# Two groups' activations turned by transfers instead of by TensorE, gates made later, weights tested in 8 bits

## What is computed

```
# experts (after the first layernorm); ensembles holds an expert's number per key, weights its share
h = relu(einsum('edi,bsi->bsed', proj_in, x))     # 8 experts, 256 -> 512
o = einsum('eid,bsed->bsei', proj_out, h)         # 512 -> 256
gate = einsum('bks,bkse->bse', weights, one_hot(ensembles, 8))
x = layernorm(x + einsum('bsei,bse->bsi', o, gate))
# feed-forward: h1_w and h2_w (the "H weights", 1024 x 1024) hold -8, 0 and 8 here
h = silu(tlin(x, w1_w, w1_s)) * tlin(x, w2_w, w2_s)
h = gelu(tlin(h, h1_w, h1_s)); h = gelu(tlin(h, h2_w, h2_s))
x = layernorm(x + tlin(h, w3_w, w3_s))
```

## Time and profile before

| | |
|---|---|
| median of 3 runs | 755.44 us (755.1 to 755.63) |
| profiled execution | 756.6 us, of which its span from the first to the last instruction is 754.8 us |
| TensorE's granted clock over the span | 0.998 |
| busy in the span | TensorE 745.3, VectorE 597.0, ScalarE 433.8, GpSimd 245.2 us |
| the first four steps (experts 0 and 1) | from about 103 to 194 us |
| the three pair passes | from about 194 to 455 us |
| the feed-forward block | from about 455 us to the end |

### The profile page before, as it was taken

The page is one execution under the profiler, slowest core; times in us unless marked ns, Lnnn a source line. Parts: engine busy times, 40 slices in busy tenths (PEclk is TensorE's granted clock), DMA queues, the critical chain, the costliest instruction groups (busy, mean ns, idle before and its releaser), DMA issues.

```text
span 754.8 us, 11840 instructions
## 1 busy us (share of the span) xinstructions
PE 745.3 (99%) x3699; PEld 630.5 (84%) x3699; DVE 597.0 (79%) x1308; ACT 433.8 (57%) x843; POOL 245.2 (32%) x278
## 2 busy tenths in 40 slices
PE   8999999999999999999999999999999999999996
PEld 6888888888888888888888888888888988888886
DVE  4789979876698999989866667894996649969466
ACT  5888743444465655556443338475676465657573
POOL 2776243233574755747443231000000300100003
PEclk9999999999999999999999999999999999999999
DMA  7900000003445345362452011035435101373201
GB/s 247 324 2 0 2 1 1 1 1 89 177 154 169 132 132 188 105 209 97 140 223 57 28 46 47 0 138 170 168 126 181 57 1 40 129 224 119 104 1 60
DMA packets 31707, 77.15 MB, mean 102 GB/s; under 512 B 8736, under 2 KB 13472, under 8 KB 27808
## 3 DMA queue, kind: packets, MB, share of 16 engines
q1 hardware_dynamic: 31360, 76.18, 29.8%
q10 hardware_dynamic: 288, 0.26, 0.2%
HBM read 58.08 MB, written 16.78 MB: 99 GB/s over the span
## 4 chain that ended last, share of the span: by engine, by line
PE 96%; DMA 1%; DVE 1%; ACT 1%; POOL 1%; issue 0%; SPq 0%; DVEq 0%; ACTq 0%
PE bank L1387 16%; PE bank L1537 13%; PE bank L1538 13%; PE bank L1236 9%; PE bank L1271 8%; PE bank L1365 8%; PE bank L1366 8%; PE bank L1370 8%; PE bank L1386 6%; PE bank L1390 2%; PE bank L1545 1%; PE bank L1544 1%; DMA wp_lo_f<-in_wproj 1%; PE bank L1254 0%; PE bank L1255 0%; PE bank L1259 0%
## 5 line engine op out<-in xcount | busy, mean ns | idle before, releaser
L1387 PE MATMUL bank<-wx_both,hx_hi 128*128 128x512 f32 x512 | 191.4, 397 | 0.0
L989 ACT ACTIVATE hx_hi<-bank 128x512 fp32r<-128x512 f32 x128 | 76.4, 597 | 175.4 <-PE bank L1370 174.2
L1537 PE MATMUL bank<-hring,wring 128*128 128x512 f32 x448 | 174.3, 389 | 0.0
L1538 PE MATMUL bank<-part_r,wring 128*128 128x512 f32 x448 | 174.3, 389 | 0.0
L720 POOL TENSOR_TENSOR x_tok<-right,x_tok 128x256 f32<-128x256 f32 x128 | 94.7, 740 | 172.0 <-ACT right L996 167.4
L2036 DVE TENSOR_TENSOR part_r<-part_f,hring 128x512 fp32r<-128x512 f32 x144 | 95.4, 686 | 42.4 <-ACT hring L1146 41.7
L1809 DVE SCALAR_TENSOR_TENSOR hx_lo<-bank,hx_hi 128x512 fp32r<-128x512 f32 x128 | 87.7, 686 | 51.4 <-ACT hx_hi L989 50.1
L1387 PEld LDWEIGHTS bank<-wx_both,hx_hi 128*128 128x128 f32 x512 | 96.0, 188 | 16.7
L1386 PE MATMUL bank<-wx_both,hx_lo 128*128 128x256 f32 x384 | 108.6, 283 | 0.0
L1538 PEld LDWEIGHTS bank<-part_r,wring 128*128 128x128 f32 x448 | 84.1, 188 | 17.5
L1537 PEld LDWEIGHTS bank<-hring,wring 128*128 128x128 f32 x448 | 84.1, 188 | 17.4
(11 more groups left out here) (209 smaller groups left out, 1415.1 us busy)
## 6 DMA issues: line engine op xcount, KB each, us to landing
wring<-h_dram SPq DMA_DIRECT2D x28, 1024.0 KB, 4.8
wx_raw<-in_wx SPq DMA_DIRECT2D x16, 512.0 KB, 7.8
raw_quads<-in_wffn SPq DMA_DIRECT2D x16, 512.0 KB, 5.7
h_dram<-sums SPq DMA_DIRECT2D x8, 1024.0 KB, 4.2
h_dram<-raw_quads SPq DMA_DIRECT2D x8, 512.0 KB, 6.6
stage<-in_wffn SPq DMA_DIRECT2D x12, 256.0 KB, 2.7
x_tok<-in_x SPq DMA_DIRECT2D x1, 2048.0 KB, 12.0
h_dram<-raw_quads SPq DMA_DIRECT2D x8, 256.0 KB, 6.8
```

The source lines that it names most:

```text
L989: act.activation(hx_hi[:, place, c], bank[b][:, :], ACT.Relu).then_inc(s_relu_ok, 1)
L1387: mm = pe.matmul(DBANK[j][:, :].rearrange("p (h d) -> p h d", h=2), hx_hi[:, place, c, a], wo_hl[:, :, c], start=(c == 0), stop=(c == XC - 1))
L1537: pe.matmul(into[:, :], w, b_hi[:, k], start=(k == 0 and i in (0, 1, 3)), stop=False, skip_group_check=True)
L1538: mm = pe.matmul(into[:, :], w, b_lo[:, k], start=False, stop=(k == KH - 1), skip_group_check=True)
```

## The change

1. **x of groups 2 and 3.** TensorE keeps only `turned(1)`. ScalarE splits the normalized rows into half words (`split_rows`), in the second half of step g for group g + 2; SP issues four transposing transfers a group; ScalarE joins the words (`joined_words`) and rounds them to the high part (`high_words`) in the first half of the next step; VectorE takes the low part from the joined words (`low_words`). VectorE makes the sums and statistics of group g + 2 in the first half of step g and normalizes it at beat 1 of the second half (`rows_normed`), and GpSimd makes the root between the halves. Group 1 is normalized and turned as before.
2. **Gates.** Steps 0 and 1 make no gates in their first halves. Expert 2's are made in the first halves of steps 2 and 3, experts 3 and 4 in the first pair pass, 5 and 6 in the second, and expert 7's in the second as well, one more on every other beat.
3. **Tests.** The four raw blocks of each quad are tested to be whole numbers of 8 bits, instead of three blocks and four sums for the short form: 32 tests, two a unit at beats 1 and 2. GpSimd's sums no longer wait for a test; SP's load of a quad waits for all four tests of the quad before the last.
4. VectorE's loop over steps 0 and 1 is unrolled.

```diff
@@ names and tiles
-CHECKED = QUADS * PRODUCTS
+CHECKED = QUADS * 4
-        rounded = at_r("rounded", o_w + 57344, [2, PIECE])
+        x_halves, x_sides = at("x_halves", o_w + 16384, [J, 2, D], U16), at("x_sides", o_w + 20480, [J, 2, DC, S], U16)
+        x_words = at("x_words", o_w + 24576, [DC, N])
+        whole, unequal = at("whole", o_w + 57344, [2, PIECE], I8), at("unequal", o_w + 58368, [PIECE])
@@ SP
+            for g in range(2, G):
+                for j in range(J):
+                    sp_.wait_ge(s_x_halves, (g - 2) * J + j + 1)
+                    sp_.dma_start_transpose(x_sides[:, j].rearrange("p h c s -> p (h c) s"), x_halves[:, j].rearrange("p h d -> p (h d)")
+                                            ).then_inc(s_x_sides, 16)
             load_expert(0, 2, 7)
...
-                    sp_.wait_ge(s_sum_cmp, PRODUCTS * (n - 2) + 3 + 2)
+                    sp_.wait_ge(s_sum_cmp, 4 * (n - 1) + 2)
@@ GpSimd
+                if further:
+                    root(g + 2)
                 for j in range(J):
-                    if further and j == 2:
-                        root(g + 2)
                     right_added(g * 2 + 1, g, j)
...
-                        pool.wait_ge(s_sum_cmp, PRODUCTS * (n - 1) + 2)
@@ ScalarE
+            def split_rows(g):
+                for j in range(J):
+                    act.wait_ge(s_xn_ok, g * J + j + 1)
+                    act.activation(x_halves[:, j], x_tok[:, g * J + j].bitcast(U16).rearrange("p (d h) -> p h d", h=2), ACT.Copy).then_inc(s_x_halves, 1)
+
+            def joined_words(g):
+                act.wait_ge(s_x_sides, (g - 1) * J * 16)
+                for j in range(J):
+                    act.activation(x_words[:, :, j * S:j * S + S].bitcast(U16).rearrange("p c (s h) -> p c s h", h=2),
+                                   x_sides[:, j].rearrange("p h c s -> p c s h"), ACT.Copy).then_inc(s_x_words, 1)
+
+            def high_words(g):
+                for j in range(J):
+                    act.wait_ge(s_x_words, (g - 2) * J + j + 1)
+                    act.activation(xT_hi[:, :, bass.ds((g * J + j) * S, S)], x_words[:, :, j * S:j * S + S], ACT.Copy).then_inc(s_xThi_ok, 1)
...
+                    if c == 1 and front and g > 0:
+                        joined_words(g + 1)
                     if c == 2 and front:
-                        halves_x(g + 1)
+                        halves_x(g + 1) if g == 0 else high_words(g + 1)
...
+                    if c == 2 and g < G - 2:
+                        split_rows(g + 2)
...
-                if i >= 3:
-                    act.wait_ge(s_sum, ((p - 1) * 4 + n) * 4 + (2, 1, 3, 4)[i - 3])
-                act.wait_ge(s_sum_cmp, ((p - 1) * 4 + n) * PRODUCTS + i + 1)
-                act.activation(rounded[:, (n * PRODUCTS + i) % 2], checked(n, i), ACT.Copy).then_inc(s_sum_rounded, 1)
+                act.wait_ge(s_sum_cmp, ((p - 1) * 4 + n) * 4 + i + 1)
+                act.activation(whole[:, i % 2], raw_quads[:, n % 2, i], ACT.Copy).then_inc(s_sum_rounded, 1)
...
-                        if not last and c < (3 if u % 2 == 0 else 4):
-                            round_checked(p, u, c if u % 2 == 0 else 3 + c)
+                        if not last and c < 2:
+                            round_checked(p, u, u % 2 * 2 + c)
@@ TensorE
-                    if n % 2 == 0 and n < 2 * G - 2 and c == 3:
+                    if n == 0 and c == 3:
                         turned(n // 2 + 1)
@@ VectorE
+                def low_words(g):
+                    for j in range(J):
+                        dve.wait_ge(s_xThi_ok, g * J + j + 1)
+                        cols = bass.ds((g * J + j) * S, S)
+                        dve.tensor_tensor(xT_lo[:, :, cols], x_words[:, :, j * S:j * S + S], xT_hi[:, :, cols].bitcast(F32), ALU.subtract).then_inc(s_xTlo_ok, 1)
...
+                def rows_normed(g):
+                    norm_apply(lambda j: group_row(g, j), lambda j: group_row(g, j), g, s_rstd_ok, s_xn_ok)
+
                 def step(g, front, further):
                     for c in range(XC):
                         if c == 3 and front:
-                            halves_x(g + 1)
+                            halves_x(g + 1) if g == 0 else low_words(g + 1)
                         low(g * 2 + 1, 1, c, c % 2)
-                        if c == 0 and front:
-                            norm_apply(lambda j: group_row(g + 1, j), lambda j: group_row(g + 1, j), g + 1, s_rstd_ok, s_xn_ok)
+                        if c == 0 and g == 0:
+                            rows_normed(1)
+                        if further:
+                            rows_added(g + 2, c)
                         gated(g * 2, g, c, 0)
-                        for e in range(2, 4):
-                            gate(g * J + c, e, masked_late[:, c * 2 + e - 2])
+                        if not further:
+                            for i in range(2):
+                                gate((g - G + 2) * 2 * J + c * 2 + i, 2, masked_late[:, c * 2 + i])
                     for c in range(XC):
                         low(g * 2 + 2, 0, c, c % 2)
-                        if further:
-                            rows_added(g + 2, c)
+                        if further and c == 1:
+                            rows_normed(g + 2)
                         gated(g * 2 + 1, g, c, 1)
...
-                with dve.Fori(0, G - 2) as g:
+                for g in range(G - 2):
                     step(g, True, True)
...
+                    dve.wait_ge(s_sum_cmp, t + 2)
+                    dve.scalar_tensor_tensor(out=unequal[:, :], in0=raw_quads[:, n % 2, i], scalar=1.0, in1=whole[:, i % 2],
                                              op0=ALU.mult, op1=ALU.not_equal, accum_out=neq[:, t:t + 1]).then_inc(s_sum_cmp, 1)
...
-                            if c == 0 and u % 2 == 0 and t > 0 and (not last or u == 0):
-                                compare(t - 1)
-                            if c > 0 and not last:
-                                compare(t + (0 if u % 2 == 0 else 3) + c - 1)
+                            if 0 < c < 3 and not last:
+                                compare(((p - 1) * 4 + u // 2) * 4 + u % 2 * 2 + c - 1)
...
-                                gate(u * 2 + c // 2, p * 2 + 2 + c % 2, masked_late[:, c])
+                                gate(u % G * J + c, p * 2 + 1 + u // G, masked_late[:, c])
+                            if p == 2 and c % 2 == 0:
+                                gate(u * 2 + c // 2, E - 1, masked_late[:, 4 + c])
```

More of the change, by code:

```diff
@@ L12 @@
 U16 = mybir.dt.uint16
+I8 = mybir.dt.int8
 ALU = mybir.AluOpType
@@ L249, in decoder_kernel @@
         s_xT_mm = sem("xT_mm")
+        s_x_halves = sem("x_halves")
+        s_x_sides = sem("x_sides")
+        s_x_words = sem("x_words")
         s_xThi_ok = sem("xThi_ok")
@@ L351, in quad @@
             return divmod(n, KH)
-        CHECKS = [("block", 0), ("block", 2), ("block", 3), ("sum", 0), ("sum", 1), ("sum", 2), ("sum", 3)]
-        def checked(n, i):
-            kind, at_ = CHECKS[i]
-            return (raw_quads if kind == "block" else sums)[:, n % 2, at_]
         A1, B1 = bank[0:4], bank[4:8]
@@ L1876, in compare @@
                 def compare(t):
-                    n, i = divmod(t, PRODUCTS)
+                    n, i = divmod(t, 4)
                     dve.wait_ge(s_sum_rounded, t + 1)
-                    a = rounded[:, t % 2]
-                    dve.scalar_tensor_tensor(out=a, in0=checked(n, i), scalar=1.0, in1=a.bitcast(F32),
+                    dve.wait_ge(s_sum_cmp, t + 2)
+                    dve.scalar_tensor_tensor(out=unequal[:, :], in0=raw_quads[:, n % 2, i], scalar=1.0, in1=whole[:, i % 2],
                                              op0=ALU.mult, op1=ALU.not_equal, accum_out=neq[:, t:t + 1]).then_inc(s_sum_cmp, 1)
@@ L1910, in pair @@
                                 dve.tensor_scalar(wide_flag[0:1, :], bank[5][0:1, 0:1], 0.0, None, ALU.is_gt).then_inc(s_wide_f, 1)
-                            t = ((p - 1) * 4 + u // 2) * PRODUCTS
-                            if c == 0 and u % 2 == 0 and t > 0 and (not last or u == 0):
-                                compare(t - 1)
-                            if c > 0 and not last:
-                                compare(t + (0 if u % 2 == 0 else 3) + c - 1)
+                            if 0 < c < 3 and not last:
+                                compare(((p - 1) * 4 + u // 2) * 4 + u % 2 * 2 + c - 1)
                             if c < 2 and last and u < 6:
```

## The result

The changed kernel takes 756.43 us, median of 22 runs (755.42 to 760.61), against 755.55 for 22 runs of the kernel before beside them (754.78 to 756.55). The ratio is 1.0026, 95% interval 1.0016 to 1.0037: a little slower. "No change" at 755.0 us was forecast; the time lies in the range, the sign is wrong.

A forecast was written before the change was run, and what follows sets the result against it. TensorE, busy 745.3 of 754.8 us, was taken to bound the kernel. The terms -1.78 + 1.0 + 0.3 = -0.48 us took the median from 755.44 to 755.0 us, range 753.6 to 757.4.

The forecast's parts named there:

- "No change" at 755.0 us: Whole kernel: terms sum to -0.48 us, median 755.44 becomes 755.0, within the 0.2% told as the same; same 0.70.
- transposes off TensorE: Groups 2 and 3: sixteen transposes leave the bounding engine, 2 x 0.89 = 1.78 us saved.
- step 0, sums ahead of the low halves: First up product of group 1: VectorE's sums delay the low halves, TensorE waits 1.0 us (0.95 to 1.3).
- step 1, low words: Group 2's up product: low words meet GpSimd's addition and end late, 0.3 us of stall (0 to 0.75).
- gates, tests, unrolled loop: Gates and tests lie under the unbroken beat, unrolling is straight-line code: worth nothing.
- beat of passes 1 to 4: TensorE's up and down product together take 2.77 us; 101 beats stay unbroken after the change.
- no stall at group 3: Step 2: VectorE has gates instead of sums, chain over 0.7 us shorter, so no stall.
- SP's later load: Block load up to 1.9 us later, expert weights land at 292.3, first read at 296.44: hidden.
- no join waited for a transfer: ScalarE's joins: group 2's last transfer lands about 1 us before; late landing was a rival, 756.4 us, chance 0.07.
- the unbroken row of 101 beats: From 159.44 to 438.88 us: 2.767 us each, no stall long enough to break the row.
- any break in passes 2 to 4: Named as a sign of a wrong forecast, since every edit there was counted at nothing.
- up to 1.58 us: VectorE's cost for an H test while GpSimd sums; worth nothing on the path, the beat being already whole.

The follow-up runs named there:

- sums_late: Changed kernel with one of group g + 2's four sums ahead of the low parts of x, two behind at beat 3, the fourth in the second half: 754.68 us.
- gates_tests: Kernel before with only the new gate placing, new tests and VectorE's unrolled loop; groups 2 and 3 stay on TensorE: 756.15 us, ratio 1.0002.
- after_nops: Changed kernel with 48 empty instructions at the head of TensorE's queue: 756.52 us.
- sums_apart: Changed kernel with the sums of rows 2 and 3 of group g + 2 at beat 3, behind the low parts of x: 755.68 us, ratio 0.9998.
- before_five: Kernel before with five unread additions more on VectorE in step 3, ahead of a low part: 757.15 us.
- tick: Changed kernel with one 1x1 TensorE matmul more at the start of step 2, behind both stalls: 756.49 us.
- sums_tick_nops: sums_apart with one 1x1 TensorE matmul more at the start of step 1 and 48 empty instructions: median 755.02 us.
- before_stall: Kernel before with six unread VectorE additions of 128x512 more in step 3, ahead of a low part: six runs, 758.31 to 763.49 us.
- before_xlow: Kernel before with one unread VectorE addition more ahead of the low part of x of group 3: 756.03 us.

## Why the prediction failed

| term (us) | forecast | measured |
|---|---|---|
| transposes off TensorE | -1.78 | -1.8 to -1.9 |
| step 0, sums ahead of the low halves | +1.0 | +0.96 |
| step 1, low words | +0.3 (0 to 0.75) | +0.6 |
| gates, tests, unrolled loop | 0 | 0 (ratio 1.0002) |
| feed-forward block | 0 (not mentioned) | +0.64 (+0.3 to +0.7 in the variants) |
| beat of passes 1 to 4 | 0 | 0, or +3.6 in 9 of 22 runs |
| time outside the span | 0 (not mentioned) | +0.2 |

The first row is read from sums_late, which has no stalls: 352.61 us from the first relu to the last down pair, against 354.41 in gates_tests and 354.51 before. The lower group of the changed kernel lies 0.65 above the kernel before, and after_nops, profiled in that group, accounts for it: 354.26 us from the first relu to the last down pair, 0.25 less than before (the first four rows give -0.22); 0.65 more in the feed-forward block; and 0.2 more of what a run takes beyond its span, 2.0 us in the median against 1.82. Together +0.6. Where the 0.2 come from is open. For sums_late the same count gives -1.9 + 0.67 + 0.2 = -1.0; it measured 754.68 against 755.79, -1.11.

**Right.** The gain of the transposes; the stall of step 0 and its cause, VectorE's chain; no stall at group 3; the gates, the tests and SP's later load hidden; no join waited for a transfer (landing 2.4 to 2.6 us).

**Mis-sized.** Step 1, +0.3 forecast and +0.6 measured. TensorE came to its low part when forecast. Four joins took 2.33 us to the next relu (131.37 to 133.70), 0.58 each and not 0.53, so the low words began 0.2 us later; the collision then cost 0.55 us (1.88 for four low words, not 1.33), a little less than the count took for it; and TensorE lost another 0.13 us behind the wait, where the last two matmuls of the product took 0.58 us to the next one (138.63 to 139.21) and not 0.45. The forecast had no term for that last part.

**Failed.** Two steps. First, the sum ends with the passes: the feed-forward block was left at nothing without a reason, and it took 0.64 us more. With step 1's 0.3 and the 0.2 outside the span it makes the sign: -0.48 was forecast, and the lower group, which the slow beat does not explain, lies at +0.65.

Second, the step that read the unbroken row of 101 beats as a property of the code: "any break in passes 2 to 4" was named as what would refute it, but the beat itself was taken as fixed. There is no break. The same matmuls run in one of two beats, and in the profiles it changes from one to the other at a wait of TensorE. So a stall, measured at 0.6 us, costs 0.033 us more in each of a hundred beats behind it in a part of the runs: 0.2 us of the median (756.43 against 756.20 for the lower group), but 1.5 us of the mean. In the kernel before, the transposes of group 3 came after every wait of pass 1; its one group of runs and its profile have the fast beat behind them. The change took them away and put a wait in their place.

That the median lies in the range is in part luck: 13 of 22 runs fell into the lower group, and the other nine lie above 759 us, outside it.

**A reading.** The "up to 1.58 us" of a test is the mean of 24 in the earlier trace rows. Nothing hangs on it, as the tests lie under the beat.

**Overlooked.** The instructions taken from TensorE's queue moved a later fetch of its code. 32 fewer (16 transposes and their weight loads, as the profile pairs them) are 3.2 us at 28 matmuls and weight loads a beat, an estimate, and the fetch came 3.7 us later: from 0.1 us ahead of the first issue to 3.6 us behind it, into the transfers. Why 48 empty instructions did not move it back is open. The profile's page counts 28 such packets with 0.46 MB, 16 KB each. The Trainium skill (Advanced Engine Details and Errata, "ISA Cache") gives a line of 16 KB, 256 instructions; the 16 KB agree, and the 256 no run here counts.

**Open.** Why there are two beats: the trace has only the spacing, 0.227 or 0.233 us. Why a wait of 0.2 us at the head of an up product set the slow one in sums_apart, if it did (that is inferred from the one group of sums_late without it), while 0.8 us there did not in nine runs of before_five. And why the upper runs of sums_apart lie only some 2 us above the lower, where a slow beat throughout would give 3.9: only one was profiled.

## What to carry to other kernels

A row of matmuls without a break can still go at two speeds, so look at the spacing, not only at the waits, and at all runs, not at the median: two groups mean that something is left to chance. Work moved ahead of what TensorE waits for is best cut where the engine's slack is; two sums moved behind the low parts of x turned this change from a loss into a gain of 1.1 us. Where instructions leave a queue, look at what its later fetches now meet.

## What the runs showed of the hardware

- TensorE's 512-column matmuls started every 0.227 or every 0.233 us at the same granted clock of 1.00, for 300 us on end. A wait could change it either way (tick: slow behind the first, fast behind the second). A 1x1 matmul without a wait ended the slow one (sums_tick_nops: 2.800 us a beat ahead of it, 2.767 behind it), and behind transposes without a wait only the faster was seen.
- Where a fetch of 16 KB of instructions fell amid four transposing transfers (eight profiles), one of the four issues took 1.82 to 2.45 us instead of 1.27 and the feed-forward block 0.3 to 0.7 us more; where it came within 0.6 us of the first (ten profiles), none of the four took more than 1.77 us and the block took no longer.
- At the start of the kernel a matmul of 40 columns took as long as one of 128 (218 ns in the trace), 48 empty instructions moved no fetch, and 40 increments of a semaphore took 5.3 us.
- VectorE's addition of two 128x512 tiles took 1.07 us to the next in one place (six in 6.4 us, before_stall) and 0.6 in another (before_xlow).
